# Reordering the steps of a fused attention and feed-forward block, with more rounds whose extra work runs on the two 64-row halves of the matmul array

## What is computed

```python
x = x + attn(layernorm(x)) + ffn(layernorm(x))

# attn: 16 heads of 16
u, v, q, k = split(silu(xn @ W1 + b1), 4)
attn = silu(einsum("bqhd,bkhd->bhqk", q, k)) / S        # S = 1024
y = layernorm(einsum("bhqk,bkhd->bqhd", attn, v) * u, gamma, beta) @ W2 + b2

# ffn: 256 -> 1024 -> 256, ternary weights
h = gelu(layernorm(xn, g1, b1) @ tern(w1).T + fb1)
out = layernorm(h, g2, b2) @ tern(w2).T + fb2
```

## Time and profile before

| what | value |
|---|---|
| device time, median of 3 runs | 1486.42 us (1486.26 to 1486.9) |
| the profiled execution: device time | 1484.9 us |
| the profiled execution: span | 1483.0 us |
| granted TensorE clock, mean | 0.999 of full speed |
| PE / ACT / DVE / POOL busy share of the span | 98% / 81% / 61% / 7% |
| HBM traffic over the span | 82 GB/s |

### The profile page before, as it was taken

One profiled execution on the slowest core, in us unless ns is written; L12 is line 12 of the kernel. 1 busy time (PEld: TensorE's weight loads), 2 busy tenths in 40 slices (PEclk: granted clock), 3 DMA queues, 4 the chain that ended last, 5 costly groups with the idle time before them and its releaser, 6 DMA issues.

```text
span 1483.0 us, 27631 instructions
## 1 busy us (share of the span) xinstructions
PE 1446.0 (98%) x10686; PEld 794.6 (54%) x10686; DVE 910.6 (61%) x1752; ACT 1207.8 (81%) x1273; POOL 97.4 (7%) x197
## 2 busy tenths in 40 slices
PE   8999999999999999999999999999999999999988
PEld 7445555555555555554555555554555456554544
DVE  5567755576545865468654775557764577556655
ACT  4788888888788887887878878888888888888875
POOL 2001000010000100001000010000100000000000
PEclk9999999999999999999999999999999999999999
DMA  7251042410524106240143303342033510415100
GB/s 245 72 143 57 16 135 65 129 58 15 157 75 104 51 17 169 84 129 3 48 138 112 103 1 83 118 135 65 1 106 95 142 58 16 128 59 142 29 2 29
DMA packets 68003, 123.60 MB, mean 83 GB/s; under 512 B 12832, under 2 KB 14496, under 8 KB 66976
## 3 DMA queue, kind: packets, MB, share of 16 engines
q1 hardware_dynamic: 67712, 121.57, 29.3%
q10 hardware_dynamic: 160, 0.26, 0.1%
HBM read 79.84 MB, written 41.94 MB: 82 GB/s over the span
## 4 chain that ended last, share of the span: by engine, by line
PE 87%; DVE 5%; ACT 5%; DVEq 1%; issue 1%; DMA 0%
PE outs L1158 30%; PE scores L1140 21%; PE fill L1278 7%; PE fill L1296 6%; PE fill L1312 4%; PE fill L1305 4%; PE fill L1244 3%; PE fill L1328 3%; PE fill L1287 3%; PE fill L1209 3%; ACT attn L672 3%; DVE st L860 1%; ACT hid L717 1%; PE fill L1268 1%; DVE hid L947 1%; DVEq L889 1%
## 5 line engine op out<-in xcount | busy, mean ns | idle before, releaser
L672 ACT ACTIVATE attn<-scores 128x1024 f32<-128x1024 f32 x1024 | 991.7, 1025 | 225.2 <-PE scores L1140 220.0
L1158 PE MATMUL outs<-attn,V 128*32 128x512 f32 x4096 | 493.8, 600 | 11.1 <-DVE uz L884 11.1
L1140 PE MATMUL scores<-QS,KS 64*128 64x512 f32 x2048 | 399.5, 452 | 14.5 <-ACT attn L672 14.0
L1140 PEld LDWEIGHTS scores<-QS,KS 64*128 64x128 f32 x2048 | 170.7, 184 | 307.3 <-ACT attn L672 232.3
L1158 PEld LDWEIGHTS outs<-attn,V 128*32 128x32 f32 x4096 | 107.7, 109 | 241.6 <-issue 241.5
L947 DVE SCALAR_TENSOR_TENSOR hid<-fill,ratq,fb1b 128x512 f32<-128x512 f32 x128 | 96.1, 751 | 74.1 <-PE fill L1296 69.4
L976 DVE TENSOR_TENSOR tmp<-fill,l2g 128x512 f32<-128x512 f32 x122 | 84.4, 691 | 65.7 <-PE fill L1305 58.4
L609 POOL TENSOR_TENSOR rp<-mv,epst 128x2 f32<-128x2 f32 x64 | 12.6, 197 | 1266.6 <-DVE mv L864 890.5
L983 DVE TENSOR_TENSOR hgl<-tmp,hgh 128x512 fp32r<-128x512 f32 x122 | 84.4, 692 | 9.2 <-issue 0.2
L1278 PE MATMUL fill<-xp,W1h 128*128 128x512 f32 x256 | 86.5, 419 | 0.5 <-DVE xp L1010 0.5
L989 DVE SCALAR_TENSOR_TENSOR part<-fill,cq,part 128x256 f32<-128x256 f32 x96 | 46.4, 483 | 56.7 <-PE fill L1244 28.4
(11 more groups left out here) (151 smaller groups left out, 1735.0 us busy)
## 6 DMA issues: line engine op xcount, KB each, us to landing
QS<-q_scratch SPq DMA_DIRECT2D x254, 128.0 KB, 3.1
k_scratch<-kst SPq DMA_DIRECT2D x64, 256.0 KB
q_scratch<-qst SPq DMA_DIRECT2D x64, 256.0 KB
KS<-k_scratch SPq DMA_DIRECT2D x128, 128.0 KB, 3.1
KS<-k_scratch SPq DMA_DIRECT2D x256, 64.0 KB, 3.3
out_dram<-part SPq DMA_DIRECT2D x15, 512.0 KB, 2.7
xin<-in_x SPq DMA_DIRECT2D x7, 1024.0 KB, 4.9
xin<-in_x SPq DMA_DIRECT2D x2, 512.0 KB, 4.2
```

The lines of the kernel that those rows point to most:

```text
L672: nc.scalar.activation(attn_of(g)[:, 2 * hf:2 * hf + 2, :], SP[:, 2 * hf:2 * hf + 2, :], ACT.Silu).then_inc(s_silu, 1)
L1140: ins = mm(SP[:, j, :], KS[rows, pair, t * P:(t + 1) * P], QS[rows, pair - c * PPC, h * HALF:(h + 1) * HALF], start=True, stop=True)
L1158: ins = mm(OP[32 * j:32 * j + 32, :], V[:, t, c * HPC // 2 + j, o * DH:o * DH + 2 * DH], attn_of(g)[:, n, :], start=(o == 0 and t == 0), s ...
```

## The change

The table of steps is written anew, and with it the one of the last batch. Below is the order by rounds (two rows of `TABLE` each), before on the left, after on the right. A star marks a round whose pieces run in halves, a plus a round with one piece on the full array ahead of a pair in halves. Before there are 6 such rounds, after 11.

The code that goes with it:

```diff
 LAST_ROUNDS = {
-    19: "ln2.2 f2.2",
-    20: "g.3.0 g.3.1 nrm2.2",
-    21: "f2.3",
-    22: "g.4.0 g.4.1",
-    23: "f2.4",
-    24: "g.5.0",
-    25: "g.5.1 gelu.3 f2.5 zs.0 zt.0 zt.1",
-    26: "ln2.3 a.0",
-    27: "nrm2.3 g.6.0 zs.1",
-    28: "g.6.1 a.1",
-    29: "f2.6",
-    30: "g.7.0 g.7.1",
+    22: "",
+    23: "nrm2.2 f2.3",
+    24: "g.4.0 g.4.1",
+    25: "f2.4 gelu.3 g.5.0 g.5.1 ln2.3 nrm2.3 zs.0 zt.0 zt.1",
+    26: "f2.5 a.0",
+    27: "g.6.0 g.6.1 zs.1",
+    28: "f2.6 a.1",
+    29: "g.7.0",
+    30: "g.7.1",
     31: "",
 }
...
+SETUP_ROUNDS = 5
+DELAYED = [s for g in range(2 * SETUP_ROUNDS) for s in SLOTS[g] if s[0] in FILLERS and s[0] not in POST and not is_next(s)]
...
 def steps_of(b, n):
...
+    if b == 0 and n == SETUP_ROUNDS:
+        for s in DELAYED:
+            yield 0, s
     for g in (2 * n, 2 * n + 1):
         for s in SLOTS[g]:
             x = b + 1 if is_next(s) else b - 1 if s[0] in POST else b
-            if 0 <= x < NB:
+            if 0 <= x < NB and not (b == 0 and n < SETUP_ROUNDS and s in DELAYED):
                 yield x, s
...
 def pieces_of(b, n):
     pieces = [xs for xs in steps_of(b, n) if xs[1][0] in FILLERS]
-    return ([], pieces) if paired(pieces) else (pieces, [])
+    for ahead in range(2):
+        if paired(pieces[ahead:]):
+            return pieces[:ahead], [], pieces[ahead:]
+    return [], pieces, []
...
             def body(b):
                 for n in range(ROUNDS):
-                    full, group = pieces_of(b, n)
+                    ahead, full, group = pieces_of(b, n)
...
+                    for x, s in ahead:
+                        step(x, *s)
                     for hf in range(2):
                         scores(b, 2 * n + 1, hf)
```

More of the change, by code:

```diff
@@ L61 @@
 TABLE = (
-    "zt.0",
-    "zs.0 zt.1",
-    "",
[L65 to L70, removed]
+    "zs.0 zt.0 zt.1 zs.1",
+    "zt.2",
+    "a.0",
+    "",
+    "zs.2 a.1",
     "",
-    "px y.1 u.1.1 u.1.0",
+    "k.1.0 q.1.0",
     "",
-    "k.1.0 q.1.0 y.0",
-    "",
-    "u.0.0",
-    "",
-    "",
-    "k.1.1",
-    "q.1.1",
-    "",
-    "u.0.1 y.2",
-    "f1.0.0",
-    "",
-    "f1.0.1 f1.1.0 f1.1.1 f1.2.0 f1.2.1 gelu.0 y.3 ln2.0 f1.3.0",
+    "a.2",
+    "",
+    "",
+    "zs.3 zt.3 u.0.0",
+    "",
+    "a.3",
+    "u.1.1",
+    "px u.0.1",
+    "k.1.1 q.1.1 y.0 y.2 y.1",
+    "",
+    "u.1.0",
+    "",
+    "f1.0.0 f1.0.1",
+    "vs.1",
+    "f1.1.0 f1.1.1",
+    "f1.2.0 y.3 f1.2.1 gelu.0 ln2.0 f1.3.0",
     "f1.3.1",
@@ L91 @@
     "",
[L92 to L96, removed]
+    "",
+    "f1.5.0 f1.5.1 gelu.1 ln2.1 f1.6.0 f2.0",
+    "",
+    "g.1.0 g.1.1",
+    "f1.6.1",
+    "",
+    "ln1 nrm2.1 f2.1",
+    "xn.0",
+    "",
+    "g.2.0 xt.0 xn.1 g.2.1",
+    "xt.1 f1.7.0",
+    "xn.2",
+    "",
+    "k.0.0 gelu.2 f1.7.1 f2.2 g.3.0 g.3.1 ln2.2",
+    "q.0.0",
     "",
     "",
-    "ln1 g.2.1 f1.7.1",
+    "nrm2.2 f2.3",
     "",
[L101 to L104, removed]
-    "",
-    "g.4.0 g.4.1",
-    "xt.1",
-    "xn.2 f2.4 xt.2",
-    "",
[L110 to L117, removed]
-    "",
[L119 to L123, removed]
-    "",
-    "vs.0 f2.7",
+    "g.4.0 g.4.1 xt.2",
+    "f2.4 xn.3 gelu.3 g.5.0 g.5.1 v.0",
+    "ln2.3 v.1 nrm2.3",
+    "",
+    "f2.5",
+    "g.6.0",
+    "g.6.1 xt.3 v.2",
+    "",
+    "f2.6",
+    "v.3 g.7.0 vs.0",
+    "",
+    "",
+    "g.7.1 k.0.1 q.0.1",
+    "",
+    "f2.7",
 )
@@ L198, in pieces_of @@
     pieces = [xs for xs in steps_of(b, n) if xs[1][0] in FILLERS]
-    return ([], pieces) if paired(pieces) else (pieces, [])
+    for ahead in range(2):
+        if paired(pieces[ahead:]):
+            return pieces[:ahead], [], pieces[ahead:]
+    return [], pieces, []
 SUM_IN_HALVES = True
 PIECES = [xs for xs in SEQUENCE if xs[1][0] in FILLERS]
-HALVED = {xs for b in range(NB) for n in range(ROUNDS) for xs in pieces_of(b, n)[1]}
-CROSSED = [pieces_of(b, n)[1][0] for b in range(NB) for n in range(ROUNDS) if pieces_of(b, n)[1]]
+HALVED = {xs for b in range(NB) for n in range(ROUNDS) for xs in pieces_of(b, n)[2]}
+CROSSED = [pieces_of(b, n)[2][0] for b in range(NB) for n in range(ROUNDS) if pieces_of(b, n)[2]]
 CROSSED = [(x, s) for x, s in CROSSED if s[0] in ("k", "u", "f1")]
@@ L217 @@
 assert len(PLACE) == len(PIECES) and len(set(SEQUENCE)) == len(SEQUENCE) == NB * len(ORDER) - len(FINISH)
-assert not any(xs[0] == 0 and xs[1][0] in FILLERS for n in range(5) for xs in steps_of(0, n))
+assert not any(xs[0] == 0 and xs[1][0] in FILLERS for n in range(SETUP_ROUNDS) for xs in steps_of(0, n))
 def in_order(*steps):
@@ L724, in body @@
                     steps = list(steps_of(b, n))
-                    group = pieces_of(b, n)[1]
+                    group = pieces_of(b, n)[2]
                     behind = steps.index(group[0]) if group else len(steps)
@@ L1373, in body @@
                             times_v(b - 1, GROUPS + g)
+                    if b == 0 and (0, PIECES[len([s for s in OPENING if s[0] in FILLERS])][1]) in ahead + full + group:
+                        pe.wait_ge(s_setup, 4)
+                    for x, s in ahead:
+                        step(x, *s)
                     for hf in range(2):
                         scores(b, 2 * n + 1, hf)
-                    if b == 0 and (0, PIECES[len([s for s in OPENING if s[0] in FILLERS])][1]) in full + group:
-                        pe.wait_ge(s_setup, 4)
                     for x, s in full:
```

## The result

The changed kernel takes 1496.0 us (median of 4 runs, 1494.37 to 1496.57) against 1486.54 of the kernel before in the same job: ratio 1.0065, 95% interval 1.0053 to 1.0077. It is 9.5 us slower. The forecast was 1488.9 with a range of 1479 to 1499, so the range holds it. But the forecast itself, no change, is not what came: it is slower, and the prediction had given "no change" and "slower" the same chance, 0.38. The profiled execution is the fastest of the four, 1494.37 us.

A forecast was written before the change was run, and what follows sets the result against it. PE, busy 98%, was the engine to watch, its rounds bound by floor, work or nearby gelus. Batches 1 to 6 -3.6, batch 0 +1.3, last batch with tail +4.7 give +2.4: 1488.9 us, called no change, range 1479 to 1499.

The forecast's parts named there:

- The prices and the floor: PE rounds: short ones take 4.82 us, longer full-array ones 3.46 plus pieces; a pair of six-matmul pieces takes 5.83, saving 0.33.
- Halves alone decide: Rival, faster: five more rounds in halves at 0.33 over eight batches, -13, 1473 us; chance 0.24 together with another faster rival.
- The gelu walk: ACT's waits around gelus: rounds 11/12 take 13.4, 15/16 13.13, 21/22 14.2 us, with stalls of 0.65, 0.3 and 1.0.
- The row's price of 1.28 us a load: ACT table loads near gelus: 1.28 us each by the profile row, where the skill page gives 2.66 a switch with a drain.
- Round 27: 3.46 + 0.80 + 0.40 + 1.37 = 6.03: Round 27 of batches 1 to 6: full-array base plus its pieces, g.6.1, xt.3 and v.2, 6.03 us.
- Round 25 ... 0.08 as in the old round 25: Round 25 of batches 1 to 6: pieces sum to 8.87 us, plus 0.08 carried from the old round 25.
- more ACT or DVE stalls: Rival, slower: extra table loads stay on the path, 1.6 us more in rounds 21/22 times 8, 1501; half, 1495; chance 0.18.
- The last batch: Last batch: rounds 0 to 18 minus 4.1, 19 to 31 plus 9.1 us; DVE's chain before a.0 makes round 26 about 11.8.
- Round 30: Round 30: k/q pair 5.83, g ahead 0.40, unseen change of array form 0.15, late silu 0.3; 6.67 us.
- late keys: Rival, slower: KS loads land late for `scores` of group 4; 1 us late in seven passages gives +7, 1496 us; chance 0.2.

The follow-up runs named there:

- Experiment 5: Changed kernel with the order of steps kept but no round in halves, all pieces on the full array: 1506.01 us against the changed kernel's 1496.0.
- experiment 3: Changed kernel with xt.3 moved from round 27 to 26, so f2.5 runs on the full array with a single evacuation: 1490.94 us against 1496.0.
- Experiment 4: Changed kernel with gelu.2 directly behind gelu.1 in round 15, sharing one pair of table loads: 1505.95 us against 1496.0.
- experiment 1: Changed kernel with zs.0, zt.0 and zt.1 ahead of ln2.3 and nrm2.3 in the last batch: 1491.06 us against 1496.0.
- experiment 8: Changed kernel with another table for the last batch (f2.3 in round 22, zs and zt ahead of ln2.3, other pieces moved): 1486.92 us against 1496.0.
- experiment 6: Changed kernel without the piece ahead of a pair, so round 30 runs its three pieces on the full array: 1501.61 us against 1496.0.
- experiment 2: Changed kernel with v.2 moved from round 27 to round 29: 1496.98 us against 1496.0.
- experiment 7: Changed kernel with the order of the KS loads of k.0.1 turned round, those group 4 needs issued 2.7 us later: 1519.96 us against 1496.0.

## Why the prediction went as it did

- **The prices and the floor** held. Rounds on the full array came out at 3.46 plus their pieces within 0.1 where nothing waits, the floor at 4.82, pairs of six-matmul pieces at 5.83 to 5.89. Experiment 5 confirms that such a pair saves 0.24 to 0.33.
- **Halves alone decide** is refuted: 10 us for all eleven rounds, not 29. Page and runs meet in part. The Trainium skill, "TensorEngine Tiling (Array Packing)", "Key Properties", has a drain at each change of mode, and the 0.33 of a lone pair fits that. What experiments 3 and 5 show is where it can be had. The same page, under "PSUM Bottleneck", warns that tiling doesn't speed up evacuation; experiment 5 agrees, where round 27 gets 0.67 shorter once f2.5 has one bank to evacuate and not two.
- **The gelu walk** held: 13.15, 13.13, 14.18 for 13.4, 13.13, 14.2, and 32 table loads into gelu in place of 24. Experiment 4 shows that the extra loads did not make the kernel slower: without them it loses more. The row's price of 1.28 us a load carried these sums, with no drain beside it.
- **"Round 27: 3.46 + 0.80 + 0.40 + 1.37 = 6.03" and "Round 25 ... 0.08 as in the old round 25"** are the steps that failed: 6.91 and 9.29 measured. They priced PE's work and put DVE's queue at nothing, or at the 0.08. The walk was made for gelu rounds, where I looked for it; rounds 25 to 28 were taken for rounds of PE. The sign was there in the rows: the old rounds 25 and 26 together took 13.99 for 13.70, and of these 0.29 the sum carried over only the 0.08 of round 25. Over batches 0 to 6 the two rounds are 8.4 us too long in sum, before small gains; between the forecast of 1488.9 and the 1496.0 measured lie 7.1. That the second evacuation and xt.3 in round 27 are the cause there, experiments 3 and 5 show; of round 25 only half is accounted for. It is the rival "more ACT or DVE stalls", right in its sign, in another place than the one it named; that its half, 1495, lies so near to the result is chance, and the range held because it was 20 us wide.
- **The last batch** was right in its mechanism (+5.0, +5.9 measured), which experiments 1 and 8 confirm. Round 26 was mis-sized, 13.6 for 11.8: the chain of DVE ends 0.5 later than it was put, and a.0 then ran at half clock, 1.5 us, which the sum did not have. Part of this is hidden, by luck, in a round 31 of 3.67 for 4.74, which has no account here.
- **Round 30**: 6.67 forecast, 6.52 measured. Over 5.83 + 0.40 that is 0.29, for which the forecast had 0.15 and 0.3; no run parts the two. What it did not see is that without the g ahead and the halves the round would take 7.20, where its pieces want 6.56 (experiment 6).
- **The start**: 1.0 us, not forecast (first `times_v` at 37.82 for 37.51, round 1 of batch 0 at 7.05 for 6.39) comes with a clock at half for 6.8 us there in place of 3.4. Nearly all profiles of the changed order have it and two have 3.4; the code up to there does the same, and whether the order causes it is not settled.

## What to carry over

When a table of steps is reordered, add up each engine's work over the stretch between two of its deadlines, not only the bound engine's work per round: a queue that is full on DVE hands its wait on from round to round, and moving the waiting piece gained nothing (experiment 2), while one evacuation less gained at once (experiments 3 and 5, round 27). A cheaper form of a matmul that needs a second evacuation is worth it only where the evacuating engine has room. And the order for the last batch is a schedule of its own: with little PE work in it, what stands first in the queue of another engine decides.

## What the runs showed that I had not expected

- A wait of PE costs more than its length. After 4.9 us of waiting in round 26 the granted clock was at 0.5 for 3.4 us, and 12 matmuls took 2.85 us in place of 1.37; in experiment 7 seven waits of 2.5 us, 17 us, were followed by 5.8 us more in the rounds behind them. Waits of that length did not always bring it: some batches of the same run went on at full clock.
- One wait can move between rounds and keep its size: in experiments 1 and 8 the sum of rounds 25 and 26 of the last batch stayed at 15.5 us, whichever of the two held it.
- The rival that the profile of the changed kernel seemed to rule out, late keys, turned up in three of the other profiles. A cover of 0.5 to 0.7 us in one execution says little about the next.
